# Attention output turned by VectorE block transposes instead of TensorE transposes, in a two-phase attention kernel on Trainium2

## The reference

```python
def _L0(x, emb, mask, ...):            # softmax attention, H=16 heads of 32
    xn = layer_norm(x, norm_w, norm_b)
    q, k = xn @ q_w + q_b, xn @ k_w + k_b
    att = softmax(einsum('bnhl,bmhl->bnmh', q, k) + (1.0 - mask) * -1000000.0, axis=2)
    v = (xn @ v_w + v_b) * mask
    y = einsum('bnmh,bmhl->bnhl', att, v).reshape(B, T, D)
    scale, shift = split(silu(emb) @ emb_w + emb_b, 2)
    h = layer_norm(y, sb_norm_w, sb_norm_b) * (1.0 + scale) + shift
    return x + silu(h) @ out_w + out_b

def _L1(x, emb, mask, ...):            # linear attention, 8 heads of 64
    xn = _ln(x, ln_w, ln_b)
    q, k = softmax(xn @ Wq + bq, heads), softmax(xn @ Wk + bk, positions)
    v = (xn @ Wv + bv) * mask
    y = q @ (k.T @ v)                  # per head
    hh = _ln(y, ln2_w, ln2_b) * (1.0 + scale) + shift
    return x + silu(hh) @ W_out + b_out
```

## Time and profile before

| what | us |
|---|---|
| median of 3 runs | 2714.92 |
| lowest and highest run | 2713.74 and 2716.24 |
| span of the profiled execution (first to last instruction) | 2713.8 |
| PE busy | 2637.9 (97%) |
| DVE busy | 1795.0 (66%) |
| POOL busy | 1348.0 (50%) |
| ACT busy | 1251.9 (46%) |

### The profile page before, as it was taken

The page is one execution under the profiler, slowest core; times in us unless marked ns, Lnnn a source line. Parts: engine busy times, 40 slices in busy tenths (PEclk is TensorE's granted clock), DMA queues, the critical chain, the costliest instruction groups (busy, mean ns, idle before and its releaser), DMA issues. The chain is left out here.

```text
span 2713.8 us, 44011 instructions
## 1 busy us (share of the span) xinstructions
PE 2637.9 (97%) x13890; PEld 1938.0 (71%) x13890; DVE 1795.0 (66%) x3213; ACT 1251.9 (46%) x2097; POOL 1348.0 (50%) x634
## 2 busy tenths in 40 slices
PE   7999999999999999999999889999999999999999
PEld 5666666666666666666663778888888888888887
DVE  6666666666666666666665777666667777766765
ACT  3555555555555555555554333333333333333233
POOL 1666666666666666666663243444434333343343
PEclk9999999999999999999999899999999999999999
DMA  6656665666566656666664401111111111111110
GB/s 146 98 85 104 99 99 83 103 99 99 84 102 99 99 83 101 99 98 89 93 114 133 156 28 51 47 51 51 51 51 51 47 47 35 43 42 43 47 35 32
DMA packets 114915, 211.44 MB, mean 78 GB/s; under 512 B 12408, under 2 KB 14508, under 8 KB 114876
## 3 DMA queue, kind: packets, MB, share of 16 engines
q1 hardware_dynamic: 78012, 143.81, 22.9%
q10 hardware_dynamic: 36864, 67.13, 18.7%
HBM read 74.87 MB, written 34.18 MB: 40 GB/s over the span
## 5 line engine op out<-in xcount | busy, mean ns | idle before, releaser
L942 DVE TENSOR_REDUCE negmax<-max_bank 128x1 f32<-128x512 f32 x1024 | 681.7, 688 | 249.2 <-PE max_bank L535 247.6
L806 ACT ACTIVATE probs<-exp_bank 128x512 f32<-128x512 f32 x1024 | 588.3, 597 | 511.9 <-PE exp_bank L550 442.5
L297 POOL TENSOR_TENSOR probs_sum<-probs_sum,probs 128x2048 f32<-128x2048 f32 x124 | 571.7, 4610 | 51.0 <-ACT probs L806 48.7
L297 POOL TENSOR_TENSOR probs_sum<-probs 128x2048 f32<-128x2048 f32 x63 | 288.5, 4579 | 503.6 <-ACT probs L806 503.6
L535 PE MATMUL max_bank<-k_stack,q_stack 98*128 98x512 f32 x1024 | 415.4, 414 | 18.9 <-DVE negmax L942 16.0
L550 PE MATMUL exp_bank<-q_stack,k_stack 100*128 100x512 f32 x1024 | 421.7, 421 | 3.2 <-ACT probs L806 3.0
L535 PEld LDWEIGHTS max_bank<-k_stack,q_stack 98*128 98x128 f32 x1024 | 189.8, 189 | 136.4 <-issue 54.4
L550 PEld LDWEIGHTS exp_bank<-q_stack,k_stack 100*128 100x128 f32 x1024 | 193.2, 189 | 123.0 <-issue 42.8
L1601 POOL TENSOR_TENSOR sT_lo<-silu,sT_hi 128x512 fp32r<-128x512 f32 x124 | 167.7, 1373 | 172.3 <-DVE sT_hi L1719 172.3
L561 PE MATMUL y_bank<-probs,v_sb 128*32 128x512 f32 x2048 | 249.6, 605 | 0.0
L1346 PE MATMUL b_work<-ident,area 128*128 128x128 f32 x1536 | 192.6, 280 | 16.9 <-DVE area L1687 9.9
(11 more groups left out here) (209 smaller groups left out, 5330.2 us busy)
## 6 DMA issues: line engine op xcount, KB each, us to landing
q_stack<-q_stage ACTq DMA_DIRECT2D x128, 256.0 KB
k_stack<-k_stage ACTq DMA_DIRECT2D x128, 256.0 KB
x_sb<-in_x SPq DMA_DIRECT2D x16, 1024.0 KB, 5.6
q_stack<-q_stage SPq DMA_DIRECT2D x64, 256.0 KB
k_stack<-k_stage SPq DMA_DIRECT2D x64, 256.0 KB
yT_scratch<-y_stage SPq DMA_DIRECT2D x64, 256.0 KB
area<-yT_scratch SPq DMA_DIRECT2D x16, 1024.0 KB, 5.2
area<-in_x SPq DMA_DIRECT2D x64, 256.0 KB, 2.8
```

Of the source, the lines that this page charges most:

```text
L297: eng.tensor_tensor(probs_sum[:, :, :], so_far, probs[:, mt, :, :], ALU.add).then_inc(probs_added, 1)
L806: act.activation(probs[:, mt, j, :], exp_bank[k % 2][:, :], ACT.Exp).then_inc(exp_done, 1)
L942: dve.tensor_reduce(negmax[:, m:m + 1], max_bank[m % 2][:, :], AXX, ALU.max, negate=True).then_inc(max_done, 1)
```

## The change

Phase one stores y in blocks: the scratch array becomes `[row, q, j, l, g, (t a)]`, where a position is 128 t + 32 q + a (q the quarter of 32 within each 128) and a feature is (j, g, l). ScalarE's copy writes the columns in the order (q, t, a), and the store writes, for each of 128 partitions, four pieces of 128 floats where it was one of 512. Phase two loads quarter q of y onto partitions 32q to 32q+31 with a DMA of its own, so four DMAs and the sums' in place of two. A tile of 128 positions then needs only each 32x32 block turned: four VectorE transposes of 128x512 a row, written into `yn` in SBUF; the scaling works on `yn` in place. PE keeps the four small transposes of the sums. In the ring the letter "-" keeps A's four places empty; the semaphore counts are worked out anew (`counts`, `Use`). SP's next `load_y` now waits for DVE's transposes and the sums.

```diff
-                sp.dma_start(yT_dram[b].rearrange("(j g l) t -> g j l t", j=HG, g=NG)[g], y_stage[:, g % 2, :]).then_inc(y_stored[g % 2], DMA)
+                sp.dma_start(yT_dram[b].rearrange("q j l g r -> g (j l) q r")[g],
+                             y_stage[:, g % 2, :].rearrange("p (q r) -> p q r", q=BLOCKS)).then_inc(y_stored[g % 2], DMA)
...
-                act.activation(y_stage[:, g % 2, :], y_bank[:, :], ACT.Copy).then_inc(y_read, 1)
+                act.activation(y_stage[:, g % 2, :].rearrange("p (q t a) -> p q t a", q=BLOCKS, t=TT),
+                               y_bank[:, :].rearrange("p (t q a) -> p q t a", t=TT, q=BLOCKS), ACT.Copy).then_inc(y_read, 1)
...
-        ORDER = (tiles_of("KL") + [("V", 0), ("V", 1)] + tiles_of("A") + [("V", 2), ("V", 3)] + tiles_of("MSH")
+        START = tiles_of("SCX")
+        ORDER = (tiles_of("KL") + [("V", 0), ("V", 1)] + tiles_of("-") + [("V", 2), ("V", 3)] + tiles_of("MSH")
...
-                sp.dma_start(yT_sb, yT_dram[b].rearrange("(g p) t -> p g t", p=P)).then_inc(y_in, DMA)
-                sp.dma_start(sums_sb[:, :], sums_dram[b]).then_inc(y_in, DMA)
+                for q in range(BLOCKS):
+                    at = slice(q * BLOCK, (q + 1) * BLOCK)
+                    sp.dma_start(y_blocks[at, :].rearrange("l (j r) -> l j r", j=HG), yT_dram[b][q].rearrange("j l g r -> l j (g r)")
+                                 ).then_inc(y_in, DMA)
+                sp.dma_start(sums_sb[:, :], sums_dram[b]).then_inc(sums_in, DMA)
...
-                        sp.wait_ge(work_full, use(kind, b, "A", TT - 1)[1] + 1)
+                        sp.wait_ge(y_turned, TT * (b + 2))
+                        sp.wait_ge(sums_turned, b + 2)
                         load_y(b + 2)
...
-                V(kind, b, (0, 1))
+                V(kind, b, (0,))
+                if kind != "last":
+                    await_sums(b + 1)
+                V(kind, b, (1,))
...
-                    A(kind, b, b + 1)
+                    turn_sums()
                 V(kind, b, (2, 3))
...
             def A(kind, b, row):
+                def turn_blocks(tt):
+                    dve.transpose(yn[:, tt, :].rearrange("p (c l) -> p c l", l=BLOCK), y_block(tt)).then_inc(y_turned, 1)
+
+                def scale_heads(tt):
+                    dve.wait_ge(y_turned, TT * row + tt + 1)
+                    heads = yn[:, tt, :].rearrange("p (h l) -> p h l", h=H0)
+                    dve.tensor_tensor(heads, heads, rinv0[:, tt, :].unsqueeze(2).broadcast_to([P, H0, DH0]), ALU.mult
+                                      ).then_inc(y_scaled, 1)
+
+                def stats_of(tt):
+                    dve.wait_ge(y_scaled, TT * row + tt + 1)
+                    return dve.bn_stats(stats[:, tt, :], yn[:, tt, :])
+
+                dve.wait_ge(y_in, DMA * BLOCKS * (row + 1))
+                if kind == "mid":
+
+                    dve.wait_ge(work_full, use(kind, b, "L", TT - 1).full + 1)
+                turn_blocks(0)
                 dve.wait_ge(sums_turned, row + 1)
                 dve.reciprocal(rinv0[:, :, :], sums_bank[:, 0:TT * H0].rearrange("p (t h) -> p t h", t=TT)
                                ).then_inc(rinv0_done, 1)
+                turn_blocks(1)
                 dve.wait_ge(rinv0_done, row + 1)
-                normalised_heads(kind, b, "A",
-                                 lambda tt: rinv0[:, tt, :].unsqueeze(2).broadcast_to([P, H0, DH0]),
-                                 "p (h l) -> p h l", dict(h=H0), "y0", row)
+                scale_heads(0)
+                turn_blocks(2)
+                scale_heads(1)
+                stats_of(0)
+                turn_blocks(3)
+                scale_heads(2)
+                stats_of(1)
+                scale_heads(3)
+                stats_of(2)
+                stats_of(3).then_inc(ln_step["y0"], 1)
+                aggregate("y0", row)
...
-    yT_dram = nc.dram_tensor("yT_scratch", (B, D, T), F32, kind="Internal").ap()
+    yT_dram = nc.dram_tensor("yT_scratch", (B, BLOCKS, HG, DH0, NG, TT * BLOCK), F32, kind="Internal").ap()
```

More of the change, by code:

```diff
@@ L17 @@
+from collections import namedtuple
 from contextlib import ExitStack
@@ L34 @@
 HG = P // DH0
+BLOCK = 32
+BLOCKS = P // BLOCK
 NG = KT
@@ L1198, in order_of, with counts @@
             return [u for u in ORDER if not (kind == "first" and u[0] in "LM")]
-        PER_ROW = len(ORDER)
-        assert PER_ROW % RING == 0
-        def use(kind, b, what, tile):
-            if kind == "start":
[L1206 to L1210, removed]
+        assert len(ORDER) % RING == 0
+        FIRST_AT = len(START)
+        ROW_AT = FIRST_AT + len(order_of("first")) - len(ORDER)
+        def counts(kind, at, tiles):
+            banks, full = [0] * RING, 0
+            for i, u in enumerate(order_of(kind)[:tiles]):
+                if u[0] != "-":
+                    banks[(at + i) % RING] += 1
+                    full += 1
+            return banks, full
+        START_READS, START_FULL = counts("start", 0, len(START))
+        FIRST_READS, FIRST_FULL = counts("first", FIRST_AT, len(ORDER))
+        ROW_READS, ROW_FULL = counts("mid", ROW_AT, len(ORDER))
+        Use = namedtuple("Use", "bank full reads")
+        def use(kind, b, what, tile):
+            order = order_of(kind)
+            n = order.index((f"end {what}" if kind == "end" else what, tile))
+            at = {"start": 0, "first": FIRST_AT}.get(kind, ROW_AT)
+            banks, full = counts(kind, at, n)
+            i = (at + n) % RING
+            if kind == "start":
+                return Use(i, full, banks[i])
+            full, reads = full + START_FULL, banks[i] + START_READS[i]
+            if kind == "first":
+                return Use(i, full, reads)
+            return Use(i, ROW_FULL * b + full + FIRST_FULL - ROW_FULL, ROW_READS[i] * b + reads + FIRST_READS[i] - ROW_READS[i])
         def bank(u):
-            return work_bank[u[0] % RING][:, :]
-        def reads(b, u):
-            return (PER_ROW // RING) * b + u[0] // RING
+            return work_bank[u.bank][:, :]
         def wait_read(eng, kind, b, what, tile):
             u = use(kind, b, what, tile)
-            eng.wait_ge(bank_read[u[0] % RING], reads(b, u) + 1)
+            eng.wait_ge(bank_read[u.bank], u.reads + 1)
         def wait_x1T(eng, kind, b):
@@ L1310, in take @@
                 u = use(kind, b, what, tile)
-                if u[0] >= RING:
-                    pe.wait_ge(bank_read[u[0] % RING], reads(b, u))
+                if not (type(u.reads) is int and u.reads == 0):
+                    pe.wait_ge(bank_read[u.bank], u.reads)
                 return bank(u)
@@ L1347, in turn, with await_sums, turn_sums @@
                 last.then_inc(work_full, 1)
-            def A(kind, b, row):
-                pe.wait_ge(y_in, 2 * DMA * (row + 1))
+            def await_sums(row):
+                pe.wait_ge(sums_in, DMA * (row + 1))
                 if not (type(row) is int and row == 0):
                     pe.wait_ge(rinv0_done, row)
[L1354 to L1360, removed]
+            def turn_sums():
+                for nt in range(TT):
+                    last = pe.transpose(sums_bank[:, nt * H0:(nt + 1) * H0], sums_sb[:, nt * P:(nt + 1) * P],
+                                        ident[0:H0, 0:H0])
+                last.then_inc(sums_turned, 1)
             def S(kind, b, row):
@@ L1660, in full @@
             def full(u):
-                dve.wait_ge(work_full, u[1] + 1)
+                dve.wait_ge(work_full, u.full + 1)
             def read(u):
-                return bank_read[u[0] % RING]
+                return bank_read[u.bank]
             def statistics(n, row, src, write, written):
@@ L1674, in statistics, with aggregate @@
                 last.then_inc(ln_step[n], 1)
+                aggregate(n, row)
+            def aggregate(n, row):
                 dve.wait_ge(ln_step[n], 3 * row + 1)
```

23 lines of the change are left out of this document (15 added, 8 removed).

## The result

| | us |
|---|---|
| changed kernel, median of 4 runs | 2750.11 (2745.66 to 2756.74) |
| kernel before beside it, median of 4 runs | 2715.58 (2713.74 to 2717.32) |
| ratio | 1.0128, 95% interval 1.011 to 1.0146 |
| profiled execution of the changed kernel | 2756.74, span 2754.9 |

The change makes the kernel 34.5 us slower; the forecast was 2756, in the range 2730 to 2786. The profiled execution is the slowest of the four, and the four stand in the order of their granted clock: 2745.66 us at 0.985, 2746.65 at 0.985, 2753.58 at 0.981, 2756.74 at 0.978.

What follows compares the result with a forecast made beforehand. It took the chain of waits from L to V 2 (10.1 us), not PE's work, as bounding. 32.2 + 2.4 + 1.5 + 4.8 = 40.9 us on the 2713.8 span gave 2754.7, as a median 2756 us, range 2730 to 2786.

Steps and rivals of the forecast that it cites:

- Removed: 0: Middle rows before V 2: taking 16 transposes, 2.29 us, off PE gains 0; the stop grows from 0.40 to about 2.7.
- The block transpose: 0.60 us: DVE in each row: four block transposes at 0.60 us each make DVE 2.4 us late, bounds 1.2 to 4.8.
- Rival 4: Block transpose on DVE is slow, 1.20 us: DVE 4.8 us late, 73.6 us in all, perhaps 2793; chance 0.15.
- The way to C: 2.3 a row, 32.2 in all: DVE's lateness passes through M 0's addition, stores, refills and sT_lo to PE's C: 2.3 us in each of 14 rows.
- the four sT_lo passes, from 2016.48, for 5.59 us: POOL before C: these passes stand behind refill 2, last 5.59 us, and move from 2016.48 to 2022.07 to 2018.9 to 2024.5.
- PE stops 2.4 us before C: Middle rows: PE waits 2.4 us there for sT_lo; less the 0.1 it already waits, 2.3 us a row.
- The clock: Half clock loses 1.6 us; hidden if it falls before V 2, costly before C, taken in 3 rows of 14: 4.8 us.
- Phase one 0: ScalarE's reordered copy and the store in 512 B pieces cost 0, or up to 5 us if they crowd stack transfers.
- The boundary 1.5: Between the phases: four y loads ahead of w_k on SP and DVE's longer chain cost 0 to 3, taken as 1.5 us.
- The first row 2.4: First row of phase two: A's chain on DVE is bare before PE's S, so DVE's lateness adds 2.4 us.
- Rival 1: PE cashes the removed transposes if V 0's addition comes earlier and POOL keeps up: about 2685 us; chance 0.04.
- Rivals 2 and 3: Second: lateness covered on both sides, about 2719, chance 0.09. Third: clock falls before C in every row, 2773, chance 0.12.

Runs made afterwards that it cites:

- number 9: Changed kernel with 16 idle PE transposes filling the stop before V 2, and POOL's low parts of S ahead of refill 2: 2723.55 us, ratio 1.0021.
- number 7: Changed kernel with V 0 and V 1 added ahead of L's last rounding, and POOL's low parts of S ahead of refill 2: 2686.32 us, ratio 0.989.
- 8: Kernel before, A's transposes kept on PE, with V 0 and V 1 added ahead of L's last rounding and POOL's low parts ahead of refill 2: 2707.54 us.
- number 4: Changed kernel with each block transpose issued twice, the extra one into an array free at that time: 2795.37 us, ratio 1.0283.
- number 5: Changed kernel with one change of POOL's order, the low parts of S ahead of refill 2: 2743.96 us, ratio 1.0101.
- number 1: Changed kernel with 16 idle TensorE transposes of the identity between V 1 and the sums, keeping PE busy before V 2: 2748.70 us, ratio 1.0113.
- number 11: Kernel before with only phase one's part of the change, the copy's column order and the store in 512 B pieces: 2715.42 us, ratio 0.9999.
- number 2: Changed kernel without the block transposes, so y is not turned and the scaling reads the loaded layout: 2742.84 us, ratio 1.0093.
- number 6: Changed kernel with one change of DVE's order, V 0 and V 1 added ahead of the rounding of L's fourth tile: 2741.75 us, ratio 1.0091.
- 3: Changed kernel with 16 idle TensorE transposes put in before the sums and the block transposes left out: 2722.70 us, ratio 1.0014.
- 10: Changed kernel with DVE's V 0 and V 1 additions and POOL's low parts of S moved earlier, each block transpose made twice: 2712.86 us, ratio 0.9979.

## Why the prediction was right

Time, sign and the main chain, DVE's lateness through M 0 to sT_lo and C, came out as forecast; where the clock costs did not. That the sum of 40.9 us lies beside the 41.1 of the profiled execution is luck: the terms for the way to C and for the clock were off and made up for each other, and phase one's 3.2 us below was no part of it. The median moved by 34.5 us.

- **Removed: 0.** Right. V 2 waits for V 0's bank, 2.54 us (2.7 forecast), still 10.1 us after L (1701.71 to 1711.80 in the chain of waits), and number 9 shows the chain from L to V 2 as the bound. The size of what lay in that wait was overstated: 2.29 us forecast, 1.83 by numbers 7 and 8. The 1.76 of twelve transposes in the earlier trace rows includes the modelled end of the last one; starts tell the pace.
- **The block transpose: 0.60 us.** Right, 0.61 to 0.62 from one start to the next, 0.59 to 0.60 by number 4. Rival 4 and the page "VectorE: DVE Perf Modes" of the Trainium skill (The three transpose paths), whose figure for 128x128 bf16 would have made 1.24 us of a tile, did not come about: f32 blocks took half of that time. DVE was 2.13 late, not 2.4, since the four scalings from SBUF save 0.02 each and the pass behind the reciprocal starts 0.22 sooner.
- **The way to C: 2.3 a row, 32.2 in all.** The chain is the one named (number 5 cuts it at refill 2), but it gives 1.76 a row (number 1), some 24 us. What failed is "the four sT_lo passes, from 2016.48, for 5.59 us": they are not of fixed length. They last 5.2 us in number 1, 5.4 to 5.6 in the changed kernel and 5.7 in number 5; what sets their length is not shown. And "PE stops 2.4 us before C" has the wrong place: in number 1 the greater part falls before Q 1, by way of S 3's silu, and in the changed kernel, whose PE comes late itself, 0.1 to 0.3 us are left of it.
- **The clock: "this loss is hidden"; 3 rows before C, 4.8 us.** This is the step that failed, though the size came near. The clock fell before V 2 in all 14 rows, and never before C. Nearly hidden it was where it is shorter than the lateness (1.6 us against 1.76; C comes 27.1 to 27.5 after V 2, with the lateness alone 27.0), not in the four long rows (2.9). By the table it adds 76.13 - 75.49 = 0.64 a row, 9 us in the profiled execution and less in the others: 0.23 through the long rows, the rest with sT_lo passes that last longer. Rows 8 had shown 0.50 for 3.15 us; that it can last 6 they had not. The page "TensorE: Matmul & The Clock Gate" of the Trainium skill (The HAM clock gate) says that idleness throttles and work restores; the 0.50 behind the stops and the 1.00 some us later agree.
- **Phase one 0:** right, by number 11. In the profiled execution it ends 3.2 us later than in that of before, which the changed code does not explain: executions with the same store end it anywhere from 1488.21 (number 7) to 1494.87 (number 11), before at 1488.78. **The boundary 1.5:** 0.7 (k product 15.10 us after phase one's last work, before 14.39). **The first row 2.4:** 2.4, plus 1.3 for half clock after its longer stop, which I had left out: the 32 transposes of S take 6.33 us, before 5.06. PE's timeline there, against the earlier trace rows:

```profile
1491.99 1.93 PE L610 MATMUL work_bank<-row_sel,k_stage 128*128 128x16 f32 x16 [0.86 <-issue]
...
1507.09 6.96 PE L1498 MATMUL b_sums_bank<-b_cols,area 128*128 128x1 f32 x32 [4.74 <-DMA area<-in_L_cond_Wk]
...
1575.91 6.33 PE L1379 MATMUL b_work<-ident,area 128*128 128x128 f32 x32 [8.93 <-DVE area L1727]
```

The account of the profiled spans: 3.2 + 0.7 + 2.4 + 1.3 to the first middle row's V 2, then 13 x 2.39 = 31.1 and 2.4 for the last, 41.1 us, all of it. Of a row's 2.39 us, 1.19 (1.76 + 1.82 - 2.39) could as well be booked to the clock as to DVE, since either alone costs them. Rival 1's conditions, V 0's addition earlier and POOL keeping up, are number 7, which took 2686.32; but its 2685 was 2.29 us of transposes a row, and number 7 gains 1.83 from the transposes and 0.67 from the stops that the two orders remove (73.73 to 73.06). Two slips change nothing: the sum for a transpose of 0.80 us comes to 2767.8, not 2769, and the 13 rows of before are alike to 0.13 us (73.68 to 73.81), not to the hundredth. Rivals 2 and 3 are excluded by the rows. Open is what decides whether and for how long the clock falls: stops of 2.54 us were followed by 3 us at half, by 6, and in five rows (one in number 5, four in number 4) by none.

## What to carry to other kernels

Work that lies inside a wait costs nothing, and taking it out gains nothing, may cost clock, and moves its price to whatever engine does it now: before moving work off a busy engine, ask which wait it fills. When the bound is two chains that meet in a row, move both: each order alone left 2742 to 2744 us, together 2686. Two delays of one consumer did not add here; the later one counted, so removing one of them showed only the small difference.

## What the runs showed of the hardware

- Stops of PE of one length had different ends. Those of 2.54 us before V 2 halved the clock in 14 rows of 14 in the changed kernel, for about 3 us in ten and about 6 in four, in 14 of 14 in number 2, in 13 in number 5 and in 10 in number 4; those of 2.1 to 2.6 us before Q 1 in 11 of 14 in number 6. In number 4 the clock fell behind the seven longest stops before Q 1 (1.9 to 3.4 us) and not behind the seven shortest (0.6 to 1.9). Stops of 0.40 and 0.80 (numbers 1, 3 and 9) before V 2, and of 0.7 to 1.3 before Q 1 (numbers 1 and 10), did not halve it: rows and windows there read 1.00.
- VectorE turns the 32x32 blocks of 128x512 f32 in 0.61 us from one start to the next, an addition over as many columns in 0.60.
- Sixteen 128x128 transposes lengthen PE's running stream by 1.83 us (numbers 7 and 8), 0.114 each, so a tile of four costs 0.46 us there against 0.61 on VectorE. The move pays in number 7 because VectorE has idle time, not because it is quicker.
